# Convolution tables kept as three bf16 parts, gathers written out, and a dummy gather at the start

## The reference

```python
src = jnp.concatenate([edge_index[0], loop])
dst = jnp.concatenate([edge_index[1], loop])
h = x @ W
deg = jax.ops.segment_sum(jnp.ones_like(dst, dtype=h.dtype), dst, num_segments=n)
dinv = jnp.where(deg > 0, jax.lax.rsqrt(deg), 0.0)
norm = dinv[src] * dinv[dst]
msg = h[src] * norm[:, None]
out = jax.ops.segment_sum(msg, dst, num_segments=n) + b
return jax.nn.relu(out)
```

## Time and profile before

| | us |
|---|---|
| median of 3 runs | 3468.88 (3465.92 to 3471.74) |
| span of the profiled execution, first to last instruction | 3254.2 |
| between that span and the median | 214.7 |
| a1, first to last gather | 526.1 |
| a2, first to last gather | 538.5 |
| a3, first to last gather | about 546 |
| projection of g1, first layer norm to start of gathers | about 37 |

### The profile page before, as it was taken

One profiled execution on the slowest core, in us unless ns is written; L12 is line 12 of the kernel. 1 busy time (PEld: TensorE's weight loads), 2 busy tenths in 40 slices (PEclk: granted clock), 3 DMA queues, 4 the chain that ended last, 5 costly groups with the idle time before them and its releaser, 6 DMA issues. The chain is left out here.

```text
span 3254.2 us, 36466 instructions
## 1 busy us (share of the span) xinstructions
PE 2205.7 (68%) x8719; PEld 1640.4 (50%) x8720; DVE 1757.0 (54%) x4031; ACT 392.4 (12%) x835; POOL 1420.3 (44%) x1451
## 2 busy tenths in 40 slices
PE   5106994555555687655554548999978888884797
PEld 3105773444344344534343436777756666663476
DVE  7547864444444783634444453333367777777343
ACT  1002210000000320100000012222211111110132
POOL 0830006777775120177777730000027777775000
PEclk9558997777777796877767778999978887886899
DMA  3210004333332000333333310000023333331000
GB/s 106 66 40 32 0 17 121 102 101 103 104 99 70 0 0 7 99 103 99 98 101 98 100 47 8 0 0 0 1 67 105 101 103 101 105 103 49 30 16 24
DMA packets 104707, 205.51 MB, mean 63 GB/s; under 512 B 33688, under 2 KB 63307, under 8 KB 104524
## 3 DMA queue, kind: packets, MB, share of 16 engines
q0 software_dynamic: 60256, 169.56, 18.9%
q1 hardware_dynamic: 44396, 35.29, 3.6%
HBM read 187.78 MB, written 16.73 MB: 63 GB/s over the span
## 5 line engine op out<-in xcount | busy, mean ns | idle before, releaser
L546 PE MATMUL PB<-BIG,OH 128*128 x1664 | 593.9, 533 | 527.6 <-issue 514.0
L400 POOL DMA_INDIRECT BIG<-table,IDX x784 | 792.9, 1011 | 225.6 <-issue 202.5
L546 PEld LDWEIGHTS PB<-BIG,OH 128*128 128x128 f32 x1664 | 453.3, 280 | 668.2 <-issue 572.2
L1215 DVE TENSOR_TENSOR ACC<-ACC,PB 128x256 f32 x832 | 350.3, 421 | 626.7 <-PE PB L546 574.8
L381 POOL DMA_INDIRECT BIG<-table,IDX x416 | 416.6, 1002 | 119.7 <-issue 118.2
L756 PE MATMUL PB<-BIG,WA 128*128 128x264 f32 x832 | 291.2, 496 | 74.5 <-DVE ACC L1518 41.8
L756 PEld LDWEIGHTS PB<-BIG,WA 128*128 128x128 f32 x832 | 184.4, 241 | 140.4 <-DVE ACC L1518 96.4
L371 POOL COPY IDX<-SRCI 128x8 int32<-128x8 int32 x1 | 0.2, 189 | 510.5 <-issue 510.5
L1417 DVE SCALAR_TENSOR_TENSOR X<-PB,SMALL,X 128x256 f32 (+1 forms) x200 | 96.8, 484 | 218.3 <-PE PB L689 218.3
L389 POOL COPY IDX<-CSTB 128x8 int32<-128x8 int32 x2 | 0.4, 206 | 456.8 <-DMA table<-ACC 456.8
L1518 DVE TENSOR_TENSOR ACC<-ACC,PB 128x264 f32 x416 | 176.4, 424 | 39.5 <-PE PB L756 22.2
(11 more groups left out here) (339 smaller groups left out, 2708.5 us busy)
## 6 DMA issues: line engine op xcount, KB each, us to landing
BIG<-table,IDX POOLq DMA_INDIRECT x1200, 2.8
table<-ACC SPq DMA_DIRECT2D x20, 660.0 KB, 3.4
X<-in_x SPq DMA_DIRECT2D x1, 3072.0 KB
out<-X SPq DMA_DIRECT2D x4, 640.0 KB
WA<-in_L_ffn_w SPq DMA_DIRECT2D x1, 2048.0 KB
WB<-in_L_ffn_w SPq DMA_DIRECT2D x1, 2048.0 KB
BIG<-wtab SPq DMA_DIRECT2D x1, 1600.0 KB, 6.3
WA<-in_L_ffn_w SPq DMA_DIRECT2D x1, 1024.0 KB, 5.0
```

The costliest lines, as they stand in the source:

```text
L400: g.indirect_dma_start(out=GT[:, k * ROW:(k + 1) * ROW], out_offset=None, in_=table, in_offset=bass.IndirectOffsetOnAxis(ap=IDX[:, k:k + 1 ...
L546: pe.matmul(PB[k][:, 0:width], OH[:, ((q % 2) * GRP + k) * P:((q % 2) * GRP + k + 1) * P], GT[:, ds(t, width)], start=True, stop=True).the ...
L1215: v.tensor_tensor(dst, dst, PB[k][:, 0:width], ALU.add).then_inc(sem(f"{st}_acc"), 1)
```

## The change

- `parts`, a new DRAM tensor in bf16 with 768 numbers a row, takes the place of `table` for g1 and g2. A row is the fp32 row as three bf16 parts: the row rounded, the rest rounded, and the rest of that. `project_parts` makes them: ScalarE rounds twice (hi, mid), VectorE subtracts twice (rest, low). `store_parts` stores them.
- The ring for edge tiles has 32 places instead of 48 (TG = 4), each with 1536 bytes a partition. The wait before a gather of tile n is `BODY + n - 4`, and comes before every fourth gather.
- TensorE sums a slot by three bf16 matmuls into the same PSUM bank. The one-hot is bf16.
- Index columns are read where they lie. The copies to IDX are gone, and all gathers of a1, a2 and a3 are written out without loops.
- GpSimd issues one gather of row 0 of x into BIG at the start of the program and waits for it.
- SyncE's loads behind `a2_ix` wait for the last slot of a2 instead.

```diff
-TG = 6
+TG = 4
+        GT = BIG[:, 0:RING * W3 // 2].bitcast(BF16)
+        SPLIT = BIG[:, 0:NT * W3 // 2].bitcast(BF16)
+        REST1 = SW[:, 0:2 * D]
+        OHB = OH[:, 0:GRP * P].bitcast(BF16)
...
+            def store_parts(st):
+                for c in range(NC):
+                    sp.wait_ge(sem(f"{st}_lo"), (c + 1) * CH)
+                    sp.dma_start(parts[c * CW:(c + 1) * CW, :].rearrange("(t p) c -> p t c", p=P),
+                                 SPLIT[:, c * CH * W3:(c + 1) * CH * W3].rearrange("p (t c) -> p t c", c=W3)).then_inc(sem("table_stored"), 16)
+
+                    sp.wait_ge(sem("table_stored"), (GNNS.index(st) * NC + c + 1) * 16)
...
-            sp.wait_ge(sem("a2_ix"), T_GROUPS + 1)
+            sp.wait_ge(sem("a2_mm"), BODY + SLOTS)
...
+            g.memset(IDX[:, :], 0).then_inc(sem("idx_zero"), 1)
+            g.wait_ge(sem("idx_zero"), 1)
+            g.indirect_dma_start(out=BIG[:, 0:D], out_offset=None, in_=a["x"],
+                                 in_offset=bass.IndirectOffsetOnAxis(ap=IDX[:, :], axis=0)).then_inc(sem("first_gather"), 16)
+            g.wait_ge(sem("first_gather"), 16)
...
-                        g.wait_ge(sem(f"{st}_mm"), BODY + n - 2 * GRP)
-                        g.wait_ge(sem(f"{st}_ix"), i * TG + q + 1)
-                        g.tensor_copy(IDX[:, r * GRP:(r + 1) * GRP], TSRC[:, ds(n + GRP, GRP)]).then_inc(sem(f"{st}_ix"), 1)
...
+                for n in range(ET):
+                    q = n // GRP % TG
+                    if n % 4 == 0:
+                        g.wait_ge(sem(f"{st}_mm"), BODY + n - 4)
+                    k = n % RING
+                    g.indirect_dma_start(out=GT[:, k * W3:(k + 1) * W3], out_offset=None, in_=parts,
+                                         in_offset=bass.IndirectOffsetOnAxis(ap=TSRC[:, n:n + 1], axis=0)).then_inc(sem(f"tiles_in{q}"), 16)
...
-                            pe.matmul(PB[k][:, 0:width], OH[:, ((q % 2) * GRP + k) * P:((q % 2) * GRP + k + 1) * P],
-                                      GT[:, ds(t, width)], start=True, stop=True).then_inc(sem(f"{st}_mm"), 1)
+                            for part in range(3):
+                                mm = pe.matmul(PB[k][:, 0:width], OHB[:, ((q % 2) * GRP + k) * P:((q % 2) * GRP + k + 1) * P],
+                                               GT[:, ds(t + part * D, width)], start=(part == 0), stop=(part == 2))
+                            mm.then_inc(sem(f"{st}_mm"), 1)
...
+            def project_parts(st):
+
+                for n in range(NT):
+                    act.wait_ge(sem(f"{st}_mm"), AHEAD + n + 1 - CH)
+                    to_xt(st, n // CH, n % CH)
+                    if n > 1:
+                        parts_of(st, n - 2)
+                parts_of(st, NT - 2)
+                parts_of(st, NT - 1)
+
+            def parts_of(st, n):
+
+                act.wait_ge(sem("rows"), rows_before(st) + AHEAD + n + 1)
+                act.activation(SPLIT[:, n * W3:n * W3 + D], tile(ACC, n, D, ROW), ACT.Copy).then_inc(sem(f"{st}_hi"), 1)
+                act.wait_ge(sem(f"{st}_rest"), n + 1)
+                act.activation(SPLIT[:, n * W3 + D:n * W3 + 2 * D], REST1[:, (n % 2) * D:(n % 2 + 1) * D], ACT.Copy).then_inc(sem(f"{st}_mid"), 1)
...
+                def rest(t):
+                    v.wait_ge(sem("rows"), rows_before(st) + AHEAD + t + 1)
+                    v.wait_ge(sem(f"{st}_hi"), t + 1)
+                    v.tensor_tensor(REST1[:, (t % 2) * D:(t % 2 + 1) * D], tile(ACC, t, D, ROW), SPLIT[:, t * W3:t * W3 + D], ALU.subtract).then_inc(sem(f"{st}_rest"), 1)
...
+                for t in range(NT + 2):
+                    if t + 3 < NT:
+                        ln_apply(st, (t + 3) // CH, (t + 3) % CH, False)
+                    if t < NT:
+                        row(t)
+                    if 0 <= t - 2:
+                        low(t - 2)
+                    if 0 <= t - 1 < NT:
+                        rest(t - 1)
```

More of the change, by code:

```diff
@@ L369, in gather_slots @@
                 g.wait_ge(sem("table_stored"), (GNNS.index(tb) + 1) * NC * 16)
[L370 to L375, removed]
-                        g.wait_ge(sem(f"{st}_mm"), BODY + n - 2 * GRP)
[L378 to L383, removed]
+                for n in range(SLOTS):
+                    q = n // GRP % NG
+                    if n % GRP == 0:
+                        g.wait_ge(sem(f"{st}_mm"), BODY + n - 2 * GRP)
+                    k = n % BODY
+                    g.indirect_dma_start(out=G[:, k * ROW:(k + 1) * ROW], out_offset=None, in_=table,
+                                         in_offset=bass.IndirectOffsetOnAxis(ap=SRCI[:, n:n + 1], axis=0)).then_inc(sem(f"{st}_in{q}"), 16)
             def gather_tiles(tb, st):
@@ L1037, in _, with project_parts, row, low @@
             attention_columns(lambda b, k: WG[:, b * GW + D + 4 * k:b * GW + D + 4 * k + 4], CSTB[:, 0:D], CSTB[:, D:2 * D], 4, "g0_weights")
+            def project_parts(st):
+                def row(t):
+                    v.wait_ge(sem(f"{st}_mm"), AHEAD + t + 1)
+                    v.tensor_scalar(tile(ACC, t, D, ROW), PB[2 + t % CH][:, 0:D], DINV[:, t:t + 1], None, ALU.mult).then_inc(sem("rows"), 1)
+                def rest(t):
+                    v.wait_ge(sem("rows"), rows_before(st) + AHEAD + t + 1)
+                    v.wait_ge(sem(f"{st}_hi"), t + 1)
+                    v.tensor_tensor(REST1[:, (t % 2) * D:(t % 2 + 1) * D], tile(ACC, t, D, ROW), SPLIT[:, t * W3:t * W3 + D], ALU.subtract).then_inc(sem(f"{st}_rest"), 1)
+                def low(t):
+                    v.wait_ge(sem(f"{st}_rest"), t + 1)
+                    v.wait_ge(sem(f"{st}_mid"), t + 1)
+                    v.tensor_tensor(SPLIT[:, t * W3 + 2 * D:t * W3 + 3 * D], REST1[:, (t % 2) * D:(t % 2 + 1) * D], SPLIT[:, t * W3 + D:t * W3 + 2 * D],
+                                    ALU.subtract).then_inc(sem(f"{st}_lo"), 1)
+                for t in range(3):
+                    ln_apply(st, 0, t, False)
+                for t in range(NT + 2):
[7 more added lines that the diff above has]
+                        rest(t - 1)
             def project(st, width, scaled):
@@ L1082, in _ @@
             v.tensor_copy(SLI[:, :], SLF[:, 8:12]).then_inc(sem("slot_tile"), 1)
-            line.step(v, v.tensor_scalar(SMALL[:, 0:4], SLF[:, 8:12], 1366.0, None, ALU.mult))
+            line.step(v, v.tensor_scalar(SMALL[:, 0:4], SLF[:, 8:12], 2048.0, None, ALU.mult))
             line.step(v, v.tensor_copy(SMALL[:, 4:8].bitcast(I32), SMALL[:, 0:4]))
@@ L1198, in onehot @@
                 def onehot(half, first):
[L1199 removed]
+                    v.tensor_tensor(OHB[:, half * GRP * P:(half + 1) * GRP * P].rearrange("p (k n) -> p k n", k=GRP),
                                     IOTA[:, :].unsqueeze(1).to_broadcast([P, GRP, P]),
```

37 lines of the change are left out of this document (14 added, 23 removed).

## The result

The changed kernel takes 3907.48 us (3895.4 to 3914.29) against 3467.4 us for the kernel before (3450.9 to 3471.74): 1.128 times as long, with an interval of 1.124 to 1.132.

The account below looks back on a forecast made before the run. GpSimd's issue of gathers bounds a1 and a2; the new wait makes a loop through GpSimd and TensorE. Span 3254.2 + 542 - 3 - 40 + 47 - 3 = 3797 us, plus 214.7 gives 4012 us, range 3880 to 4150.

Parts of the forecast that it names:

- the dummy: Program start: the early gather moves a 47.4 us first-gather cost, -40 us; rival, it gains little, 4050 us, chance 0.12.
- the projections: Rows of g1 and g2: extra roundings and subtractions cost +23.5 us each, +47 both; low-clock rival +48, chance 0.08.
- The wait and its period: a1 and a2: GpSimd stands after every eighth gather; a 16.4 us loop against 10.3 a group, +542 us together.
- Piece 1: Loop of a1 and a2: first to last gather's start in a group, seven turns of 1.256 us, 8.8 us.
- Piece 2: Loop of a1 and a2: last gather's start until TensorE starts, 4.5 us plus 0.15 for wider rows, 4.65 us.
- Pieces 3 and 4: Loop of a1 and a2: four slots from TensorE's start to the fourth addition, 3.05 us; GpSimd resuming, 0.1 us.
- The first rival: a1 and a2: GpSimd does not wait, the new wait never binds; 3404 us, faster by 1.9%, chance 0.03.
- The high clock: Rival in a1 and a2: TensorE's burst runs at high clock, four slots in 1.7 us; -125, 3890 us, chance 0.10.
- the cost by bytes: Rival: rows of 1536 bytes make each gather take 1.45 times 0.95 us; +335, 4345 us, chance 0.06.
- The weight loads: Rival: bf16 matmuls' weight loads are not hidden, four slots cost 1.3 us more; +125, 4135 us, chance 0.13.
- The third gather of a1: Takes 7.21 us in place of 0.95 beside SyncE's weight loads, and will again: 6.3 us.
- The 214.7 us: Gap of the kernel before's median above its profiled span, added to the forecast span of 3797 us.

Follow-up runs that it names:

- b_tight: Kernel before with only the gather wait changed, slots up to n - 4 summed instead of n - 16: 4070.24 us, ratio 1.1679.
- a_half: Changed kernel with TensorE waiting for landings of four gathers at a time instead of eight: 3504.24 us, ratio 1.0055.
- a_pairs_gap: Changed kernel with waits and landings by pairs of tiles, and a VectorE pause between batches in the counting's second part: 3198.51 us, ratio 0.9805.
- b_gap: Kernel before with VectorE pausing between its one-hot batches in the counting of edges: 3244.66 us, ratio 0.9963.

## Why the prediction held, and where it did not

The forecast was 4012 us, the time 3907.48, inside the range. The forecast of the span was 3797 us from a trace on a chip without stands; on such a chip it is 3794.8. That these two lie 2 us apart is partly luck: 40 us that the dummy did not bring stand against 46 us less than forecast for the loops, the projections and a3. The sizes below are from the traces without stands.

- **The wait and its period: right.** Each stage has one idle stretch of GpSimd before each group, released by TensorE, 48 of them, 6.2 us long. Piece 1 came out at 8.9 us for 8.8. Piece 2 was mis-sized: 4.13 us for 4.65. The row of a stage's last gather (4.5 us) was taken for every eighth, with the reason that no other gather follows. `b_tight` refutes the reason: 3.88 us with none following, 3.87 in the kernel before with two or three. The last gather of a stage takes about 4.5 to 4.7 us in `b_tight` and the changed kernel too; why is open. For the wider rows I had 0.15 us, and the runs show 0.26 (3.87 to 4.13). Pieces 3 and 4 came out at 3.0 us for 3.15, at a granted clock of 0.50 for the first 2.9 us of each burst. The period is 16.05 for 16.4 us. a1 and a2 together cost +511 us for +542.
- **The first rival: refuted.** GpSimd waits 597 us.
- **The high clock and the cost by bytes: refuted.** The clock is 0.50 where that rival had full speed, and a gather of 1536-byte rows keeps GpSimd busy for 0.946 us at the median, one of 1056 bytes 0.953.
- **The weight loads: hidden.** 0.64 us a slot, as taken; that rival did not come.
- **The third gather of a1: right in size, wrong in cause.** It takes 6.82 us again. I had put the 6.3 us down to SyncE's loads. It ends 0.8 us behind VectorE's 25 operations of L1287, which read three SBUF operands:

```profile
525.62 9.98 DVE L1287 SCALAR_TENSOR_TENSOR ACC<-CSTB,T,ACC 128x256 f32 x25 [0.35 <-DVE T L1282]
526.56 1.15 POOL L405 DMA_INDIRECT BIG<-parts,CSTB  x1 [0.30 <-issue]
528.01 1.29 POOL L405 DMA_INDIRECT BIG<-parts,CSTB  x1 [0.30 <-issue]
529.60 6.82 POOL L405 DMA_INDIRECT BIG<-parts,CSTB  x1 [0.30 <-issue]
```

  In all runs the long gather of a1 and of a2 ends 0.8 us behind these operations, however long it takes: 8.40 us in `a_half`, 5.64 in a2 of `a_pairs_gap`. Why the two gathers before it run beside the same operations in 1.15 and 1.29 us is open.

- **The dummy: wrong, and its rival came (0.12).** The step that failed is the reading of 47.4 us as a one-time cost, from the one fact that only the first gather has it. I did not look at what ended when it ended. VectorE's row beside it was in the same trace. The Trainium skill, "SBUF — State Buffer", says that GpSimd and VectorE share a port pair as an exclusive lock, which VectorE takes with two SBUF inputs against a GpSimd operation that reads SBUF. In the kernel the indices of an indirect DMA lie there. The 46.69 us and the 1.15 us of `b_gap` agree. The page has the lock last for one instruction; here it was lost to GpSimd for 46 us of instructions of 1.09 us each. The same page reports that a `tensor_tensor` did not stall a DMA; the comparisons here are `tensor_tensor` and held a gather, and the measurement decides.
- **The projections: right.** The gathers of a1 start 20.9 us later, and a2's another 20.9, for +23.5 each. The rival of the low clock did not come.
- **a3: -13 us for -3**, on chips without stands. 415 turns take 1.283 us in place of 1.314. Some 8 us of it are gathers of over 1.2 us, 11 before and 2 now, which I had not counted.
- **The 214.7 us: wrong.** They were added as launch work. They are stands of the kernel before, and the change does not carry them all: in a1 and a2, where GpSimd now waits 6.2 us before every group, there are none, and what is left is 105 us in a3 and 8 elsewhere (3908.3 less 3794.8). That is 101 of the 104 us by which the forecast was too long, and the reason why the ratio is 1.128 on one kind of chip and 1.163 on the other.

## What to carry to other kernels

Tightening a ring's wait is not priced by the wait but by the loop it closes: issue a group, let it land, sum enough of it. If that loop is longer than the issue alone, count landings in smaller groups, which gave back nearly all of it here with fours and all of it with pairs. When one instruction takes 50 times its usual length, look at which other engine's work ends at the same moment before calling it a first-time cost. Put a wait for data behind the register loads that do not need it. And when a profiled span and the timed runs are 6% apart, profile the kernel again before building on either.

## What the runs showed of the hardware

- The same program takes 3260 us on two chips and 3467 to 3489 us on others. On the others VectorE waits for "remote" for up to 13.6 us, in a1, a2 and a3 alone, and ScalarE for up to 20 us in a3. They were seen wherever gathers go on at full pace. With a wait of 6.2 us in 16 (changed kernel) or 6.9 in 17 (`b_tight`) there were none in a1 and a2; in `a_half`, where GpSimd pauses for 2 us at most groups, there were. The cause is open.
- Comparisons of two bf16 SBUF operands, 896 columns in 1.09 us, back to back, held an indirect gather for 46.7 us; with 0.6 us between batches it took 1.15, and 36 of the gathers beside them 1.6 in place of 0.95. A held gather ended 0.8 to 1.0 us behind the last of these operations.
- TensorE started 3.87 us after the start of a gather of 1056-byte rows and 4.13 us after one of 1536-byte rows, and 3.3 us where its register load stood ahead of the wait. Whether other gathers followed made no difference.
